# A four-layer attention and expert-network kernel: the first expert network is entered by half 0 of two experts, each expert network ends with half 0 of its last two experts, and the following stage is begun earlier

## What is computed

```python
x -> layernorm -> attention over ctx, 16 heads       ; x += output       # layer 0
y  = layernorm(layernorm(x)) * gamma[e] + beta[e]    # its own scale and shift for each expert
x += sum over the best 2 of 8 experts:  w[e] * (relu(y @ W1[e] + b1[e]) @ W2[e] + b2[e])
...                                                  # also w[e] * normed x, with both weights
x -> 16 wide heads over ctx, then a gated MLP        # layer 1
x += best 2 of 16 experts (hidden width 256)
x -> attention that keeps 90% of the keys            # layer 2
x += best 2 of 8 gated experts: (silu(y @ Wg) * (y @ Wu)) @ Wd
x -> context-query attention, its features @ W_qv    # layer 3
x -> one network of width 512 with norm, gamma, beta
```

## Time and profile before

| | before |
|---|---|
| three runs, us | 792.15, 792.12, 788.83 (median 792.12) |
| the profiled execution, us | 792.12 |
| its span, us | 790.4 |
| mean granted clock of TensorE | 0.981 |
| PE busy, us (share) | 730.3 (92%) |
| DVE, ACT, POOL busy, us | 519.2, 460.4, 420.1 |
| DMA | 38.47 MB, 49 GB/s |

### The profile page before, as it was taken

How to read it: one execution, slowest core, us unless ns; L and a number is a source line. 1 busy time by engine, 2 the same in 40 slices (tenths; PEclk the granted TensorE clock), 3 DMA queues, 4 the chain that set the end, 5 groups by cost and what they waited for, 6 DMA issues and landing times. The chain is left out here.

```text
span 790.4 us, 14719 instructions
## 1 busy us (share of the span) xinstructions
PE 730.3 (92%) x5121; PEld 592.6 (75%) x5121; DVE 519.2 (66%) x1380; ACT 460.4 (58%) x1390; POOL 420.1 (53%) x414
## 2 busy tenths in 40 slices
PE   6988899999899999898989999989889999999896
PEld 3656797777688887776878788756668888888796
DVE  5896476776576666576656677658866366666556
ACT  3993455674687776573224777469924456665312
POOL 6854345864576654433222677476342378886311
PEclk9999899999999999999999999989999999999999
DMA  7002122220000000000003445100010232210000
GB/s 288 2 1 86 63 83 93 94 81 0 2 2 2 1 8 2 1 1 1 7 22 104 144 133 165 52 2 2 2 41 28 96 107 68 80 54 1 1 1 28
DMA packets 16361, 38.47 MB, mean 49 GB/s; under 512 B 1896, under 2 KB 6272, under 8 KB 16032
## 3 DMA queue, kind: packets, MB, share of 16 engines
q1 hardware_dynamic: 16288, 37.53, 14.1%
HBM read 36.87 MB, written 0.66 MB: 47 GB/s over the span
## 5 line engine op out<-in xcount | busy, mean ns | idle before, releaser
L1297 PE MATMUL banks<-input_hi,weights_in_lo 128*128 128x512 f32 x296 | 121.2, 409 | 4.6 <-PEq L1665 3.2
L1297 PE MATMUL banks<-input_lo,weights_in_hi 128*128 128x512 f32 x296 | 117.0, 395 | 0.0
L1297 PE MATMUL banks<-input_hi,weights_in_hi 128*128 128x512 f32 x296 | 116.4, 393 | 0.0
L1011 ACT ACTIVATE probabilities<-banks,neg_max 128x128 f32<-128x128 f32 x256 | 91.3, 474 | 12.3 <-DVE neg_max L2034 12.3
L823 POOL TENSOR_TENSOR hidden_lo<-hidden,hidden_hi 128x512 fp32r<-128x512 f32 x50 | 64.6, 1296 | 42.4 <-ACT hidden L1173 39.9
L712 POOL TENSOR_TENSOR rstd<-var_eps,neg_half 128x4 f32<-128x4 f32 x23 | 23.7, 1031 | 105.6 <-POOLq L711 85.3
L1011 ACT ACTIVATION_READ_ACCUMULATOR probabilities<-banks,neg_max 128x1 f32 x256 | 73.6, 314 | 0.0
L830 POOL TENSOR_TENSOR hidden<-hidden,scratch 128x512 f32<-128x512 f32 x48 | 62.0, 1293 | 19.3 <-ACT hidden L1159 16.7
L780 POOL TENSOR_TENSOR weights_in_lo<-weights_in,weights_in_hi 128x256 fp32r<-128x256 f32 (+2 forms) x33 | 42.7, 1295 | 53.2 <-ACT weights_in_hi L1184 52.1
L1297 PEld LDWEIGHTS banks<-input_hi,weights_in_lo 128*128 128x128 f32 x296 | 56.4, 191 | 18.5 <-issue 4.4
L1297 PE MATMUL banks<-hidden_hi,weights_out_lo 128*128 128x512 f32 x164 | 67.6, 412 | 1.2 <-POOL weights_out_lo L813 1.2
(11 more groups left out here) (297 smaller groups left out, 1831.9 us busy)
## 6 DMA issues: line engine op xcount, KB each, us to landing
scratch<-cw_rows SPq DMA_DIRECT2D x25, 512.0 KB, 3.8
weights_out<-w_in SPq DMA_DIRECT2D x17, 256.0 KB, 2.8
weights_in<-w_in SPq DMA_DIRECT2D x8, 512.0 KB, 3.7
weights_in<-w_in SPq DMA_DIRECT2D x9, 256.0 KB, 2.7
weights_in<-w_in SPq DMA_DIRECT2D x16, 128.0 KB, 2.3
weights_out<-w_in SPq DMA_DIRECT2D x16, 128.0 KB, 2.1
wq<-w_in SPq DMA_DIRECT2D x1, 1024.0 KB, 5.1
wo<-w_in SPq DMA_DIRECT2D x1, 1024.0 KB, 7.4
```

Of the source, the lines that this page charges most:

```text
L1011: act.activation(prob[:, n // 2 % 2, h, :], b8(n % (2 if prune else 3))[:, i, :], ACT.Exp, bias=neg_max8[:, n % 4, i:i + 1], accum_out=z[: ...
L1297: return pe.matmul(o, l, rh, start=start, stop=stop, **kw)
```

## The change

It has six parts.

1. **Order of steps.** `f.order` maps a step to (expert, half). In every expert network the last four steps are (e, 0), (e+1, 0), (e, 1), (e+1, 1) with e the last but one expert; in `ffn0` the first four are so too: (0, 0), (1, 0), (0, 1), (1, 1). `last_step(e)` replaces the expression 2e + 1 where a buffer is waited for.
2. **Closing.** Half 0's sum is complete two steps earlier. ACT copies it in the last but one step (`copy_sums(0)`), PE turns it in the middle of the last `hidden` (`turn_sums(f, 0)`), DVE adds it and makes statistics and norm of half 0 between its pieces of the last step (`closing`); in `ffn1` only the copy and the turning move, DVE's part keeps its place. Half 1's sum is turned behind two products of the next stage, and the projection of the context's values moves behind the transpose of half 0.
3. **Opening of the first network.** The output projection of the attention's half 0, its add and its statistics, `shift_sums`, `turn_shift`, the norm of half 0 and its transpose go into the last units of the attention. POOL splits the weights of experts 0 and 1 there too (`high_first`, `scale_first`, `low_first`). ACT no longer makes a second copy of the input; DVE subtracts from the PSUM bank (`split_entry`).
4. **First steps of the first network.** `hidden` of (0, 0) and (1, 0) come first, then everything that needs half 1: its transposes, `routing`, both `plain_output`s of half 0. The product of the normed tokens with the summed weights (`routed`) moves one step behind. SP brings expert 3's first weights and expert 2's second weights behind the rows of token weights instead of ahead of them.
5. **Stage after the third network.** `context_scores(0)` runs before half 1 is normed, with half 0's part of `row_sims` and of the projection of the features (banks 4 and 5 instead of 0 and 1), and likewise for half 1.
6. **`keep_busy` counts** are adapted; before the last network 9 instead of 16.

```diff
+                self.order = [divmod(s, 2) for s in range(2 * experts)]
+                if gamma:
+                    self.order[0:4] = [(0, 0), (1, 0), (0, 1), (1, 1)]
+                e = experts - 2
+                self.order[-4:] = [(e, 0), (e + 1, 0), (e, 1), (e + 1, 1)]
+                self.sums_turned_at = (7, 1) if gated else (5, 1)
...
                 load_first(2)
-                load_first(3)
-                load_second(2)
+                if not f.gamma:
+                    load_first(3)
+                    load_second(2)
                 sp.wait_ge(cw_rows_ready, f.at["turned"] + 2)
...
                 load_wide(f.new_from + 1)
+                if f.gamma:
+                    load_first(3)
+                    load_second(2)
...
-                                     (spread_values, batches, 3)], UNITS, 1, st.close)
+                                     (spread_values, batches, 3), (beta_columns, (0,), 14),
+                                     (lambda it, n: high_first(0), (0,), 15),
+                                     (lambda it, n: scale_first(0), (0,), 16),
+                                     (lambda it, n: high_first(1), (0,), 18),
+                                     (lambda it, n: inverse_roots((0,)), (0,), 18)], UNITS, 1, st.close)
...
+                def copy_sums(half):
+                    act.wait_ge(outputs_done, f.outputs_count(f.steps - 3 + 2 * half))
+                    act.activation(y_feat[:, 4 * half:4 * half + 4, :], b4(f.sums[half]), ACT.Copy)\
+                        .then_inc(sums_ready, 1)
...
+                        if s == f.steps - 2:
+                            copy_sums(0)
...
-                                   (first_output, (0,), 17)], UNITS, 1, lambda: None)
+                                   (first_output, (0,), 15), (shift, (0,), 15), (first_turned_back, (0,), 17)],
+                              UNITS, 1, lambda: None)
...
                     for fc in range(f.FC):
+                        if f.FC == 4 and (s, fc) == (f.steps - 1, 2):
+                            turn_sums(f, 0)
...
-                    if f.gamma and s == 0:
+                    if s == 1 and f.gamma:
                         transpose_half(1, xn, 7)
                         plain_output(0)
+                        pe.wait_ge(feat_ready, 2)
+                        transpose_half(1, source, 7)
+                        routing()
+                        plain_output(1)
+                    elif s == 1:
+                        routing()
+                    if f.gamma and s < 2:
                         continue
-                    if s == 1:
-                        routing()
+                    if f.gamma and s == 2:
+                        turn_weights()
+                        continue
...
             project(w("wk2"), ctxT, 2, (0, 1), keys_projected)
-            project_tok(w("wv2"), ctxT, 4)
+            turn_sums(ffn1, 1)
             keep_busy(7, 6)
             transpose_half(0, xn, 0)
-            keep_busy(7, 2)
+            project_tok(w("wv2"), ctxT, 4)
...
+            keep_busy(2, 5)
+            turn_sums(ffn2, 1)
+            transpose_half(0, xn, 0)
+            keep_busy(6, 8)
+            context_scores(0)
+            keep_busy(6, 4)
+            transpose_half(1, xn, 1)
+            keep_busy(6, 4)
+            context_scores(1)
...
-            keep_busy(7, 16)
+            keep_busy(7, 9)
...
                     elif f.FC == 4 and f.plain <= s < f.steps:
-                        for fc in range(3):
-                            weigh(s, fc)
+                        closing = s == f.steps - 1
+                        weigh(s, 0)
+                        weigh(s, 1)
+                        if closing:
+                            add_sums(0, f)
+                        weigh(s, 2)
+                        if closing:
+                            norm_stats(0, x, 1e-5)
                         low_part(s, 1)
                         weigh(s, 3)
                         low_part(s, 3)
+                        if closing:
+                            norm_apply(0, x, xn, norm_tok_ready)
```

323 lines of the change are left out of this document (180 added, 143 removed).

## The result

| | before | changed |
|---|---|---|
| runs, us | 788.83 to 792.15, median 791.96 (4) | 776.78 to 780.78, median 779.11 (4) |
| the profiled execution, us | 792.12 | 780.78 |
| its span, us | 790.4 | 779.1 |
| mean granted clock of TensorE | 0.981 | 0.985 |

The ratio is 0.9847, 95% interval 0.9818 to 0.9875: 12.9 us less in the median, 11.3 in the profiled executions. The forecast was 777.1 (770 to 785). Both kernels ran once more in a later comparison, with 779.16 against 790.3 us, ratio 0.9858 (0.9826 to 0.9891).

A forecast was written before the change was run, and what follows sets the result against it. PE, busy 730 of 790 us, was taken as the bound, leaving only the joints between stages to gain from. Gains of 8.3 + 0 + 1.5 + 0.35 + 4.8 = 15.0 us from 792.1 gave 777.1 us, range 770 to 785.

The forecast's parts named there:

- First product: Opening of the first network: its first product comes at 77.7 instead of 82.62, 4.9 us earlier.
- turning of the token weights: First network: token weights turned at 96.0 instead of 104.34, a gain of 8.3 us (5.9 to 9.5).
- The give-back: First network's weighted steps: 1.1 us of new DMA waits against about 1.1 of old ones, net 0 (-0.5 to +3).
- First closing: Closing of the first network: half 0 normed in the last step, scores behind it earlier, gain 1.5 us (0.8 to 2.3).
- Second closing: Closing of the second network: half 0's norm and the first query product earlier, gain 0.35 us (0 to 0.9).
- Third closing: Third closing and the stage behind it: scores by half, less chain, fewer dummies, gain 4.8 us (3 to 6).
- The sign that I gave for this closing: Third closing: distance from last output to DVE's first operation on the row sums 2.1 us shorter, no stretch below full clock.
- (a): Rival: in the first network rows or expert 3's weights land late and engines wait; 3 us, 780.1; 20%.
- (b): Rival: the clock falls all the same at the opening (2.4 us) and third closing (1.3 us); 780.8; 10%.
- (c): Rival: the closings give nothing and only the opening's gain is left; 783.8; 8%.
- (f): Rival: DVE, ACT and PE fall into lock step in the first network's 11 weighted steps, costing 20.5 us; 797.6; 4%.
- (e): Rival: more gain, the opening a microsecond earlier and the closings at their upper bounds; 772.7; 4%.

The follow-up runs named there:

- a_pow_late: Changed kernel with POOL's power for half 0 behind both splits of the first weights, as in the old order; 784.42 us.
- b_dum: Kernel before, with 13 instead of 5 unread products ahead of the transpose of the twice normed half 0; 790.11 us against 793.32.
- a_load: Changed kernel with expert 3's first and expert 2's second weights issued ahead of the token weights' rows again; 781.84 us.
- a_stats_late: Changed kernel with half 0's statistics behind the last low part in the last step of the first and third network; 781.13 us.
- a_close: Changed kernel with half 1's norm ahead of the value copies (first closing) and half 1's transpose ahead of half 0's row sums (third); 778.74 us.
- a_rows: a_close plus POOL's addition of a row of constants to the residual held back until DVE has made half 1's queries; 775.19 us.
- a_16: Changed kernel with 16 instead of 9 unread products ahead of the last network's first transpose; 781.88 us.
- a_nodum: Changed kernel without its 21 unread products in the first network's opening; 780.18 us.

## Why the prediction was right, and where it was not

- **First product (4.9, came 4.65) and turning of the token weights (8.3, came 8.23).** Right by its mechanism, with small errors in the steps that cancel: half 0's transpose 0.25 us later than stepped (70.05 instead of 69.8), the second norm's transpose 5.62 us behind it instead of 6.05, the first product 2.30 us behind that instead of 1.85. POOL's place decides the first part (a_pow_late: 3.1 us, 4.6 with the clock), and the clock is 2.3 us of the second (b_dum). That the second hidden layer covers half 1's norm is what keeps the clock's gain: in the kernel before, half 1 took 0.9 us of it back.
- **The give-back (0, came 0.1).** The number was right, but not for the reason given (1.1 us of new waits against 1.1 of old ones): two edits cancel, and it was no small term: reordering the loads is worth 3.1 us (a_load). I had treated the issue order as a matter of a microsecond either way. The step that failed is the bound by the row of 4.1 us from issue to DVE: the cost of the old order is not the landing, it is the store that stands behind an issue waiting for a buffer.
- **First closing (1.5, came 1.6).** Right, though the norm took 3.15 us instead of 1.12, held up by POOL; PE's products covered it. The last output was 0.46 us late, as forecast.
- **Second closing (0.35, came 0.1 at the first queries and 0.5 at half 1's transpose).** Right in size.
- **Third closing (4.8, came 3.55).** Of the 1.25 us that are missing, 0.9 are lost up to DVE's first operation on the row sums (1.63 earlier instead of 2.55) and 0.3 behind it. Up to it, half 1's transpose came 0.4 us earlier instead of 0.7, and half 1's queries took 0.55 us longer, held up by POOL. Ahead of both, the last output was 0.92 us late instead of 0.45, and the statistics are half of that (a_stats_late). PE reached half 1's transpose 1.6 us after it could (a_close); this by itself cost nothing, because half 1's queries then ran into the whole of POOL's operation: both together are worth 1.6 us (a_rows), and I had neither. The dummies gave 1.0 us where I had 1.2 (a_16). The sign that I gave for this closing had the wrong direction in it: with the last output 0.45 us late the distance from it should be 2.55 + 0.45 = 3.0 us shorter, and not 2.1; it came 2.55 shorter.
- **Elsewhere (0, came -2.6).** The forecast took the clock's behaviour outside the change as given, with one spell for one idle time. It is not: the same idle time gave 0, 3.4 or 6.8 us. The profiled execution of the changed kernel had bad luck there; the median of all runs was 12.9 us ahead, 1.5 more than the profile. That the total of the runs lies within 2 us of the forecast is in part luck, since the clock decides over several microseconds of it.
- **Rivals.** (a), late rows, did not happen, since the change avoided it; in a_load it did, at the 3 us that it was given. (b) did not happen: the clock was 1.00 in both places, and in a_nodum it was so in the opening with 4 unread products instead of 25. (c), no gain in the closings, fell. (f), lock step, did not come: the waits of 0.28 us at 112 and a few more add up to what they were. Two sums in the prediction don't come out as written: the upper bounds that (e) names give 773.4 us and not 772.7, and the bounds of all terms added up give 773 to 785 and not 770 to 781. The stated range of 770 to 785 holds both.

## What to carry to other kernels

Move the work of a joint into the steps before it, but look at each queue that it passes: POOL's power behind two splits (4.6 us with its clock), a small store behind an issue that waits for a buffer (3.1 us), a power one unit too early in a loop (2.8 us and the clock). Look first at PE's idle times of 1.9 us and more, for behind most of them comes a lottery over several microseconds; removing one saves it and the clock behind it, filling one with unread products saves only the clock. Single profiles of kernels with such idle times differ by 4 us for no reason in the code, so set traces against each other place by place instead of by their totals.
